# Attention sums kept by feature: denominators by DMA, the scaling on GpSimd, maxima turned by DVE

## Chip, cores and metric

The kernel runs on one core of a Trainium2 chip. The metric is the device time of one execution in microseconds.

## What is computed

A layer of attention and a recurrence, each followed by a residual sum and a layer norm, on x of shape (16, 512, 256):

```python
q = heads(x @ Wq); k_s, v_s = heads(x @ Wkv_short); k_l, v_l = heads(x @ Wkv_long)   # 16 heads of 16
decay_bias = -abs(pos[None, :] - pos[:, None]) * (1.0 - decay_factor)
out_short = attention(q, k_s, v_s, decay_bias)      # softmax(q k^T / 4 + bias) v
out_long = attention(q, k_l, v_l, None)
alpha = sigmoid(mix_weight)
x = layernorm(x + (alpha * out_short + (1 - alpha) * out_long) @ Wo)
# then, over the first axis t as time:
f = sigmoid(x_t @ wf.T + c @ uf.T + bf); i = sigmoid(x_t @ wi.T + c @ ui.T + bi); g = tanh(x_t @ wc.T + c @ uc.T + bc)
c = f * c + i * g
h = tanh(x @ wo.T + c_final @ uo.T + bo); x = layernorm(x + h)
```

## The kernel before

Attention comes first, for 16 batches b, then the recurrence. All five engines run orders written out by hand; they meet at semaphores. SP issues DMAs, GpSimd (POOL) has few instructions.

A batch is 8 units of 4 heads: unit u is head group u // 2 and attention u % 2 (0 long, 1 short). Units with u odd have the decay bias, whose diagonal part are small bf16 matmuls (L634). A unit is four slots of 128 keys, so a batch has 32 slots. In slot s PE computes the transposed scores for the exp ("b" fills, L658, in two pairs of heads), the scores of two units later, only for their row maxima ("a" fills, L684), weighs the values of the slot before with the exps (weigh, L722, sums and denominators in pv_ps, 17 rows per head: 16 features and the sum of exps), and may do a work task. ACT reads each "b" fill (exp, L391), DVE each "a" fill (maximum, L581). The fills of a unit go round three pairs of PSUM banks in the order FILLS (L107); before a fill PE waits until the fill three places back has been read (banks_free, L637). In the text b(2,0) is the "b" fill of the unit's third slot, first pair, and exp(2,0) the exp of it.

Work tasks (TASKS, L54) use the one bank `work`: "v" projects values, "kq" keys and queries (two halves; for the next batch), "wo" projects the attention output and DVE adds it to x_res (add_rows, L555), "ot" turns o_sum (L775), "turn" at slots 4m + 1. The turn of unit u - 1 transposes pv_sb, which ACT has copied from pv_ps (keep_sums, L424, after exp(0,1) of a unit), so that tokens lie on partitions; DVE takes the reciprocal of the denominators (L547) and multiplies (L551) into o_att. The same task turns the maxima of the next unit (L792); DVE negates them (L541) and SP writes them as an extra row of q_op (L304). GpSimd adds the two attentions' halves (o_sum, L332), twice per batch. "ot" makes the high part ot_h (ACT, L402) and the low part ot_l (DVE, L532), from which "wo" is made with three matmuls per product.

SP's order per batch: at slots 4m six DMAs with keys (load_k), at slots 8n + 2 six with queries (load_q), at slots 4m + 1 the maxima. GpSimd also makes xt_l, the low part of the next x (L339), which the kq tasks from slot 10 on and the x load on ACT at slot 10 (L434) wait for, and the factors of the layer norm (L345 to L350). After the last batch (L845 to L857) the first products of the recurrence are placed among the last steps of attention.

## Time and profile before

| | us |
|---|---|
| median of 3 runs | 2189.14 (2188.74 to 2189.32) |
| the profiled execution | 2190.01 |
| its span in the profile | 2188.2 |
| PE busy | 2107.5 (96%) |
| DVE busy | 1633.3 (75%) |
| ACT busy | 1470.2 (67%) |
| POOL busy | 134.4 (6%) |

The profile is of one execution. Busy time is the union of an engine's instructions; matmuls overlap, so the distance from one start to the next says what one costs. PEld are PE's weight loads. The idle time in front of an instruction stands in brackets with what released it. "SPq" and "ACTq" rows are DMA issues.

### The profile page before, as it was taken

How to read it: one execution, taken by the hardware profiler on the slowest of the kernel's cores; microseconds unless marked ns; L12 is line 12 of the kernel's file. 1: busy time of each engine (PE TensorE's matmuls, PEld its weight loads, DVE VectorE, ACT ScalarE, POOL GpSimd, SP SyncE). 2: the span in 40 equal slices, each digit the busy share in tenths (PEclk: the TensorE clock that was granted, in tenths of full speed). 3: DMA queues.
4: the chain of work that ended last, by engine and by line, in shares of the span. 5: the costliest groups of instructions: out<-in, count | busy, mean ns of one | idle time of the engine just before them, and what ended most of it. 6: DMA issues, size and time to landing. Idle time of an engine off the chain costs nothing.

```text
span 2188.2 us, 41691 instructions
## 1 busy us (share of the span) xinstructions
PE 2107.5 (96%) x16608; PEld 1139.3 (52%) x16608; DVE 1633.3 (75%) x2099; ACT 1470.2 (67%) x1766; POOL 134.4 (6%) x186
## 2 busy tenths in 40 slices
PE   6999999999999999999999999999999879999995
PEld 3444444444444444444444444444444348888873
DVE  6788888888888888888888888888888833333347
ACT  2777777777777777777777777787777653333338
POOL 0000000000000000000000000000000000000005
PEclk8999999999999999999999999999999989999998
DMA  4222222222222222222222222222222302000007
GB/s 109 55 57 55 67 55 66 55 64 55 65 56 66 56 65 56 64 56 64 56 63 64 55 64 55 64 55 64 55 55 54 91 28 69 29 20 28 29 10 259
DMA packets 91252, 134.14 MB, mean 61 GB/s; under 512 B 21301, under 2 KB 43573, under 8 KB 91077
## 3 DMA queue, kind: packets, MB, share of 16 engines
q1 hardware_dynamic: 66948, 97.91, 17.6%
q10 hardware_dynamic: 24128, 33.79, 4.8%
q8 instruction: 122, 2.00, 0.4%
q14 instruction: 54, 0.43, 0.1%
HBM read 37.77 MB, written 16.78 MB: 25 GB/s over the span
## 4 chain that ended last, share of the span: by engine, by line
PE 89%; ACT 4%; DVE 3%; issue 2%; DMA 1%; SPq 1%; ACTq 0%; POOL 0%; DVEq 0%; POOLq 0%
PE pv_ps L722 21%; PE pair_ps L658 17%; PE work L626 15%; PE banks L1176 12%; PE pair_ps L684 12%; PE work L788 3%; PE pair_ps L634 3%; ACT probs L391 2%; PE banks L1199 2%; DVE maxes L581 1%; PE banks L1233 1%; PE banks L1169 1%; PE work L792 1%; DVE res L563 1%; ACT summed L1044 1%
## 5 line engine op out<-in xcount | busy, mean ns | idle before, releaser
L581 DVE TENSOR_REDUCE maxes<-pair_ps 128x2 f32<-128x1024 f32 x1024 | 1228.0, 1221 | 240.5 <-PE pair_ps L634 153.9
L391 ACT ACTIVATE probs<-pair_ps,small 128x1024 f32<-128x1024 f32 x512 | 563.1, 1113 | 227.1 <-PE pair_ps L634 225.6
L391 ACT ACTIVATE probs<-pair_ps 128x1024 f32<-128x1024 f32 x512 | 516.8, 1024 | 160.0 <-PE pair_ps L658 154.8
L722 PE MATMUL pv_ps<-probs,vals 128*32 128x512 f32 x4096 | 547.3, 606 | 0.6 <-ACT probs L391 0.6
L658 PE MATMUL pair_ps<-q_op,k_op 56*128 56x512 f32 (+1 forms) x2048 | 479.6, 477 | 15.4 <-ACT probs L391 11.5
L684 PE MATMUL pair_ps<-k_op,q_op 55*128 55x512 f32 x2048 | 434.1, 432 | 6.7 <-ACT probs L391 4.5
L658 PEld LDWEIGHTS pair_ps<-q_op,k_op 56*128 56x128 f32 (+1 forms) x2048 | 191.7, 184 | 446.9 <-DVE maxes L581 204.7
L684 PEld LDWEIGHTS pair_ps<-k_op,q_op 55*128 55x128 f32 x2048 | 196.0, 186 | 151.4 <-issue 107.3
L634 PE MATMUL pair_ps<-eye_b,tri_b 64*128 64x64 bf16 x4096 | 163.0, 194 | 0.0
L634 PEld LDWEIGHTS pair_ps<-eye_b,tri_b 64*128 64x128 bf16 x4096 | 93.8, 96 | 114.6 <-issue 93.3
L722 PEld LDWEIGHTS pv_ps<-probs,vals 128*32 128x32 f32 x4096 | 80.7, 108 | 98.3 <-issue 87.3
L332 POOL TENSOR_TENSOR o_sum<-o_att 128x512 f32<-128x512 f32 x32 | 41.2, 1287 | 1287.9 <-DVE o_att L551 1287.9
L993 ACT ACTIVATE act_out<-banks,bias 128x512 f32<-128x512 f32 x96 | 65.9, 687 | 76.7 <-PE banks L1176 75.9
L1084 DVE TENSOR_TENSOR xs_l<-banks,xs_h 128x512 fp32r<-128x512 f32 x32 | 20.6, 685 | 104.8 <-ACT xs_h L982 104.8
L788 PE MATMUL work<-ident_sb,pv_sb 128*128 128x128 f32 x512 | 84.3, 288 | 14.3 <-ACT pv_sb L427 10.1
L626 PE MATMUL work<-xt_h,w_hi 128*128 128x512 f32 x184 | 92.6, 503 | 0.0
L427 ACT ACTIVATE pv_sb<-pv_ps 128x512 f32<-128x512 f32 x128 | 76.6, 598 | 22.3 <-PE pv_ps L722 15.3
L626 PE MATMUL work<-wv_hi,xt_h 128*128 128x256 f32 x256 | 84.7, 331 | 4.7 <-DVE w_lo L513 3.3
L982 ACT ACTIVATE xs_h<-banks 128x512 fp32r<-128x512 f32 x32 | 17.4, 595 | 105.2 <-PE banks L1169 105.2
L532 DVE SCALAR_TENSOR_TENSOR kq_l<-work,kq_h 128x512 fp32r<-128x512 f32 x92 | 63.6, 691 | 29.4 <-ACT kq_h L406 29.4
L1176 PE MATMUL banks<-xs_h,wx_h 128*128 128x512 f32 x192 | 76.1, 396 | 2.1 <-DVE xs_l L1084 2.1
L1176 PE MATMUL banks<-s_h,uc_h 128*128 128x512 f32 x192 | 77.4, 403 | 0.0
(161 smaller groups left out, 2450.5 us busy)
## 6 DMA issues: line engine op xcount, KB each, us to landing
k_op<-kq_h SPq DMA_DIRECT2D x508, 64.0 KB, 2.2
q_op<-kq_h SPq DMA_DIRECT2D x256, 64.0 KB, 2.2
k_op<-kq_l SPq DMA_DIRECT2D x254, 64.0 KB, 2.2
x_step<-in_xT ACTq DMA_DIRECT2D x16, 512.0 KB, 3.9
q_op<-kq_l SPq DMA_DIRECT2D x128, 64.0 KB, 2.2
x_res<-in_x ACTq DMA_DIRECT2D x16, 512.0 KB, 4.0
x_dram<-res ACTq DMA_DIRECT2D x16, 512.0 KB, 2.9
x_back<-x_dram SPq DMA_DIRECT2D x16, 512.0 KB, 5.4
```

The source lines that it names most:

```text
L391: act.activation(probs[:, s % 2, 2 * hp:2 * hp + 2, :], pairs_ps[pair_of(b, s, "b", hp)][:, :, :], ACT.Exp, scale=LAM if s // 4 % 2 else 1 ...
L427: act.activation(pv_sb[:, u % 2, :], pv_ps[:, :], ACT.Copy).then_inc(pv_copied, 1)
L532: dve.scalar_tensor_tensor(dst, work[:, :], scale, hi.bitcast(F32), ALU.mult, ALU.subtract).then_inc(done[kind], 1)
L581: dve.reduce_max(maxes[:, u % 2, :, hp, s % 4], pairs_ps[pair_of(b, s, "a", hp)][:, :, :], mybir.AxisListType.X).then_inc(a_reduced, 1)
L626: last = pe.matmul(out, lhs(a, k), rhs(c, k), start=(k == 0 and a + c == 0), stop=(k == KC - 1 and c == 1))
L634: yield pe.matmul(bank[:, P * chunk + HALF * half:P * chunk + HALF * half + HALF], tri_b[at:at + HALF, which, half, :], eye_b[at:at + HALF ...
L658: last = pe.matmul(banks[:, j, :], k[HALF * j:HALF * j + rows, hp, P * c:P * c + P], q[HALF * j:HALF * j + rows, hp, :], start=True, stop= ...
L684: last = pe.matmul(banks[:, j, :], q[at:at + MAX_ROW, hp, P * c:P * c + P], k[at:at + MAX_ROW, hp, :], start=True, stop=u % 2 == 0)
L722: last = pe.matmul(pv_ps[32 * h:32 * h + 32, :], vals[:, c, g // 2, att, at:at + 32], probs[:, s % 2, h, :], start=(c == 0), stop=(c == TC ...
L788: last = pe.transpose(work[:, P * t:P * t + P], pv_sb[:, sums[1] % 2, P * t:P * t + P], id_sb[:, :])
L993: act.activation(act_out[:, k, g, :], gate_ps[n], ACT.Tanh, bias=bias[:, g, k:k + 1], scale=0.5 if g < 2 else 1.0).then_inc(gate_done, 1)
L1176: last = pe.matmul(gate_ps[n], lhs[a][:, g, k, P * mc:P * mc + P], rhs[d][:, k, :], start=start and m == 0, stop=stop and m == len(parts) - 1)
```

## The change

Sums and denominators stay with features on partitions. pv_sb is copied from pv_ps as before; SP then moves its rows: the four denominators of a unit to `dens` (spread over 128 partitions, 16 each), the rows of each head to `o_att`, which is now laid out by feature: five DMAs per unit. Once per half batch (k = 0 or 1) DVE takes the reciprocal of dens (slots 3 and 19), SP stores it to DRAM (slots 4 and 20) and loads it back, each head's row repeated on 16 partitions, as `inverses` (two DMAs, slots 6 and 22). GpSimd multiplies o_att by it for both attentions and adds them to o_sum; ACT copies o_sum to ot_h (slots 9 and 25), GpSimd subtracts for ot_l. The task "ot" and the transposes of pv_sb are gone. The maxima of a unit are turned by DVE (32x32 blocks), in slot 4m, and moved by four DMAs instead of one; their sign is in the constants. PE's task "turn" is gone. "wo" stands at slots 12, 16, 20, "v" at 24, 28, 0, 2, 3, 4, 6. GpSimd's order per batch: multiply and add for k = 1 of the batch before, xt_l, ot_l for k = 1, layer norm factors, multiply and add and ot_l for k = 0. The memset of vals moves to GpSimd, the constants tri and eye are loaded into x_res.

```diff
-TASKS = {0: ("ot", 0, -1), 2: ("v", (4,), 0), 3: ("v", (5,), 0), 4: ("v", (6,), 0), 6: ("ot", 1, -1), 7: ("v", (7,), 0),
-         8: ("wo", (0,), -1), 12: ("wo", (1,), -1), 16: ("wo", (2, 3), -1), 20: ("v", (0, 1), 1), 24: ("v", (2,), 1), 28: ("v", (3,), 1)}
+TASKS = {0: ("v", (3,), 0), 2: ("v", (4,), 0), 3: ("v", (5,), 0), 4: ("v", (6,), 0), 6: ("v", (7,), 0),
+         12: ("wo", (0,), -1), 16: ("wo", (1,), -1), 20: ("wo", (2, 3), -1), 24: ("v", (0, 1), 1), 28: ("v", (2,), 1)}
 TASKS |= {10 + 4 * i + half: ("kq", (n, half), 1) for i, n in enumerate(KQ_ORDER) for half in range(2)}
 
-TASKS |= {4 * m + 1: ("turn", m, 0) for m in range(UNITS)}
+
+INVERT, STORE_INVERSES, LOAD_INVERSES, HIGH_PART = ({at: (1, -1), at + 16: (0, 0)} for at in (3, 4, 6, 9))
...
-        rden = sb("rden", [P, 2, TC, GH])
-        o_att = [sb(f"o_att{a}", [P, TC, NH, HD]) for a in range(2)]
-        o_sum = sb("o_sum", [P, TC, H])
+
+        o_att, inverses = sb("o_att", [P, 2, KC, L]), sb("inverses", [P, 2, L])
+        o_sum = sb("o_sum", [P, KC, L])
+
+        dens = sb("dens", [P, KC, 2, 2, HD])
+        inv_dram = nc.dram_tensor("inv_dram", [KC, 2, 2, GH * L], F32, kind="Internal").ap()
...
-        maxes = sb("maxes", [P, 2, 2, GH // 2, TC])
-        shift_rows = sb("shift_rows", [GH * TC, 2, P], F32R)
-
-        tri_sb, tri_b = sb("tri_sb", [P, 2, 2, P]), sb("tri_b", [P, 2, 2, P], BF16)
-        eye_sb, eye_b = sb("eye_sb", [P, HALF]), sb("eye_b", [P, HALF], BF16)
+        maxes = sb("maxes", [P, 2, 2 * GH * TC], F32R)
+        maxima = [maxes[:, a, 0:GH * TC].rearrange("p (h m c) -> p h m c", h=2, m=GH // 2) for a in range(2)]
+
+        shift_rows = sb("shift_rows", [P, 2, 2 * GH * TC], F32R)
+
+        tri_b, eye_b = sb("tri_b", [P, 2, 2, P], BF16), sb("eye_b", [P, HALF], BF16)
+        x_res_flat = x_res[:, :, :].rearrange("p t n -> p (t n)")
+        tri_sb = x_res_flat[:, 0:4 * P].rearrange("p (a f n) -> p a f n", a=2, f=2)
+        eye_sb = x_res_flat[:, 4 * P:4 * P + HALF]
...
+            def move_maxima(b, u):
+                if exists(b):
+                    wait(sp, done["shift"], b, UNITS, u + 1)
+                    row = MAX_ROW + u % 2
+                    to = q_op[u // 2][row:row + HALF + 1:HALF, :, :].rearrange("r h (t n) -> r (h t) n", n=P)
+                    for at in range(0, P, 32):
+                        copy_words(to[:, :, at:at + 32], shift_rows[at:at + GH * TC, u % 2, :]).then_inc(shift_loaded[u % 2], 16)
+
+            def move_sums(b, u):
+
+                if exists(b):
+                    g, att = u // 2, u % 2
+                    wait(sp, pv_copied, b, UNITS, u + 1)
+                    wait(sp, inv_stored, b, 16 * 2, 16 * (u // 4 - 1))
+                    sp.dma_start(dens[:, g // 2, att, g % 2, :], pv_sb[HD:P:32, att, :]).then_inc(sums_moved[att], 16)
+                    wait(sp, osum_done, b, 2, u // 4 - 1)
+                    for h in range(GH):
+                        to = HALF * (g % 2) + HD * h
+                        sp.dma_start(o_att[to:to + HD, att, g // 2, :], pv_sb[32 * h:32 * h + HD, att, :]).then_inc(sums_moved[att], 16)
+
+            def store_inverses(b, k):
+                if exists(b):
+                    wait(sp, inverted, b, 2, k + 1)
+                    for a in range(2):
+                        wait(sp, inv_loaded[a], b, 16 * 2, 16 * (k - 1))
+                    sp.dma_start(inv_dram[k].rearrange("a g (p e) -> p (a g) e", p=P), dens[:, k, :, :, :].rearrange("p a g e -> p (a g) e")).then_inc(inv_stored, 16)
+
+            def load_inverses(b, k):
+                if exists(b):
+                    wait(sp, inv_stored, b, 16 * 2, 16 * (k + 1))
+                    for a in range(2):
+                        wait(sp, scaled, b, 4, 2 * k)
+                        rows = inv_dram[k, a].rearrange("g (h n) -> (g h) n", n=L)
+                        sp.dma_start(inverses[:, a, :], rows.unsqueeze(1).to_broadcast([2 * GH, HD, L])).then_inc(inv_loaded[a], 16)
...
-                    if s in TASKS and TASKS[s][0] == "turn":
-                        _, maxima = turned(b, TASKS[s][1])
-                        if maxima:
-                            bb, u = maxima
-                            wait(sp, done["shift"], bb, UNITS, u + 1)
-                            row = MAX_ROW + u % 2
-                            copy_words(q_op[u // 2][row:row + HALF + 1:HALF, :, :].rearrange("r h (t n) -> r (h t) n", n=P),
-                                       shift_rows[:, u % 2, :]).then_inc(shift_loaded[u % 2], 16)
+                    if s % 4 == 1:
+                        move_maxima(*unit_of(b, s // 4 + 1))
+                        move_sums(*sums_before(b, s // 4))
+                    for slots, move in ((STORE_INVERSES, store_inverses), (LOAD_INVERSES, load_inverses)):
+                        if s in slots:
+                            k, off = slots[s]
+                            move(b + off, k)
...
+            move_sums(B - 1, UNITS - 1)
+            store_inverses(B - 1, 1)
+            load_inverses(B - 1, 1)
...
+            pool.memset(vals[:, :, :, :, :], 1.0).then_inc(ones_set, 1)
+            pool.memset(maxes[:, :, :].bitcast(F32), 0.0).then_inc(ones_set, 1)
...
-                def add_attentions(bb, n):
-
-                    wait(pool, done["pvt"], bb, UNITS, UNITS // 2 * (n + 1))
-                    o = [a[:, :, NH // 2 * n:NH // 2 * (n + 1), :].rearrange("p t h d -> p t (h d)") for a in o_att]
-                    pool.tensor_tensor(o_sum[:, :, P * n:P * n + P], o[0], o[1], ALU.add).then_inc(osum_done, 1)
+                def add_attentions(bb, k):
+
+                    for a in range(2):
+                        wait(pool, inv_loaded[a], bb, 16 * 2, 16 * (k + 1))
+                        pool.tensor_tensor(o_att[:, a, k, :], o_att[:, a, k, :], inverses[:, a, :], ALU.mult).then_inc(scaled, 1)
+                    wait(pool, scaled, bb, 4, 2 * k + 2)
+                    wait(pool, done["ot"], bb, 2, k - 1)
+                    pool.tensor_tensor(o_sum[:, k, :], o_att[:, 0, k, :], o_att[:, 1, k, :], ALU.add).then_inc(osum_done, 1)
+
+                def low_part(bb, k):
+                    wait(pool, ot_hi, bb, 2, k + 1)
+                    wait(pool, full["wo"], bb, 4, 0)
+                    pool.tensor_tensor(ot_l[:, k, :], o_sum[:, k, :], ot_h[:, k, :].bitcast(F32), ALU.subtract).then_inc(done["ot"], 1)
...
                                        ALU.subtract).then_inc(xt_lo, 1)
-                if exists(b):
-                    add_attentions(b, 0)
+                if exists(bb):
+                    low_part(bb, 1)
...
                 wait(act, pv_full, b, SLOTS, 4 * u + 4)
+                wait(act, sums_moved[u % 2], b, 80 * UNITS // 2, 80 * (u // 2))
                 act.activation(pv_sb[:, u % 2, :], pv_ps[:, :], ACT.Copy).then_inc(pv_copied, 1)
+
+            def high_part(b, k):
+
+                if exists(b):
+                    wait(act, osum_done, b, 2, k + 1)
+                    wait(act, full["wo"], b, 4, 0)
+                    act.activation(ot_h[:, k, :], o_sum[:, k, :], ACT.Copy).then_inc(ot_hi, 1)
...
+                    if s in HIGH_PART:
+                        k, off = HIGH_PART[s]
+                        high_part(b + off, k)
...
-            def turn(b, m):
-
-                sums, maxima = turned(b, m)
-                wait(dve, full["turn"], b, UNITS, m + 2)
-                if maxima:
-                    bb, u = maxima
-                    wait(dve, shift_loaded[u % 2], bb, 16 * UNITS // 2, 16 * (u // 2))
-                    dve.tensor_scalar(shift_rows[:, u % 2, :].rearrange("p (g e) -> p g e", e=GAP), turned_maxima, -1.0, None,
-                                      ALU.mult).then_inc(done["shift"], 1)
-                if sums:
-                    bb, u = sums
-                    g, att = u // 2, u % 2
-                    o = work[:, :].rearrange("p (t h e) -> p t h e", t=TC, h=GH)
-                    dve.reciprocal(rden[:, att, :, :], o[:, :, :, HD]).then_inc(rden_done, 1)
-                    wait(dve, rden_done, bb, UNITS, u + 1)
-                    if u < 2:
-                        wait(dve, osum_done, bb, 2, 0)
-                    dve.tensor_tensor(o_att[att][:, :, GH * g:GH * g + GH, :], o[:, :, :, 0:HD],
-                                      rden[:, att, :, :].unsqueeze(3).to_broadcast([P, TC, GH, HD]),
-                                      ALU.mult).then_inc(done["pvt"], 1)
+            def turn(b, u):
+
+
+                if exists(b):
+                    wait(dve, a_reduced, b, 8 * UNITS, 8 * u + 8)
+                    wait(dve, shift_loaded[u % 2], b, 64 * UNITS // 2, 64 * (u // 2))
+                    dve.transpose(shift_rows[:, u % 2, :].bitcast(F32), maxes[:, u % 2, :].bitcast(F32)).then_inc(done["shift"], 1)
+
+            def invert(b, k):
+
+                if exists(b):
+                    for a in range(2):
+                        wait(dve, sums_moved[a], b, 80 * UNITS // 2, 80 * (2 * k + 2))
+                    dve.reciprocal(dens[:, k, :, :, :], dens[:, k, :, :, :]).then_inc(inverted, 1)
...
+                        turn(*unit_of(b, s // 4 + 1))
                         reduce(1)
...
+                    if s in INVERT:
+                        k, off = INVERT[s]
+                        invert(b + off, k)
...
-            after.prepare(dve)
-            rest(ot_l[:, 0, :], ot_h[:, 0, :], ot_hi, "ot", B - 1, 0, 1.0)
-            turn(B, 0)
             after.step_lo(dve, 0, 0)
             after.step_lo(dve, 0, 1)
-            rest(ot_l[:, 1, :], ot_h[:, 1, :], ot_hi, "ot", B - 1, 1, 1.0)
+            invert(B - 1, 1)
+            after.prepare(dve)
...
-                    wait(pe, osum_done, bb, 2, n + 1)
-                    for t in range(TC):
-                        last = pe.transpose(work[:, P * t:P * t + P], o_sum[:, t, P * n:P * n + P], id_sb[:, :])
-                    last.then_inc(full["ot"], 1)
                 if kind == "wo":
                     wait(pe, done["ot"], bb, 2, 2)
                     for t in n:
                         at = H * (t % 2)
                         three(work[:, at:at + H], lambda a, k: (ot_h, ot_l)[a][:, k, P * t:P * t + P],
                               lambda a, k: (w_hi, w_lo)[a][:, 3, k, :]).then_inc(full["wo"], 1)
...
-                if kind == "turn":
-                    sums, maxima = turned(b, n)
-                    if sums:
-                        wait(pe, pv_copied, sums[0], UNITS, sums[1] + 1)
-                        for t in range(TC):
-                            last = pe.transpose(work[:, P * t:P * t + P], pv_sb[:, sums[1] % 2, P * t:P * t + P], id_sb[:, :])
-                    if maxima:
-
-                        wait(pe, a_reduced, maxima[0], 8 * UNITS, 8 * maxima[1] + 8)
-                        last = pe.transpose(turned_maxima, maxes[:, maxima[1] % 2, :, :, :].rearrange("p a h t -> p (a h t)"), id_sb[:, :])
-                    last.then_inc(full["turn"], 1)
 
...
-            work_task(B, 0)
             weigh_before(B, 0)
             after.turn_step(pe, 0, True)
-            work_task(B, 1)
-            after.gates_from_x(pe, 0, (0, 1), True)
-            work_task(B, 6)
-            after.gates_from_x(pe, 0, (2, 3), True)
+            after.gates_from_x(pe, 0, (0, 1, 2, 3), True)
             pe.wait_ge(done["ot"], 2 * B)
             for t in range(TC):
```

## Rows read from the trace of the kernel before

**Rows 1.** The page's fourth part: the chain that ended last, its shares by engine.
```profile
PE 89%; ACT 4%; DVE 3%; issue 2%; DMA 1%; SPq 1%; ACTq 0%; POOL 0%; DVEq 0%; POOLq 0%
```

**Rows 2.** Busy time by stretches (one batch; before the recurrence): columns in its header.
```profile
core 0: us, PE busy (x) PEld busy (x) DVE busy (x) ACT busy (x) POOL busy (x), PEclk, DMA share, GB/s
697.25:805.40 108.15, 107.17 (x928) 51.65 (x926) 90.68 (x108) 81.41 (x93) 6.54 (x7) 1.00 0.24 60
1770.00:1800.00 30.00, 22.20 (x134) 15.34 (x131) 12.34 (x31) 8.05 (x12) 2.05 (x3) 0.81 0.06 18
```

**Rows 3.** Timeline, slot 5: start us, length us, engine, line, operation, tiles, count.
```profile
930.07 2.12 ACT L391 ACTIVATE probs<-pair_ps,small 128x1024 f32<-128x1024 f32 x2 [0.17 <-PE pair_ps L634]
930.34 0.66 PE L788 MATMUL work<-ident_sb,pv_sb 128*128 128x128 f32 x4
...
931.03 1.06 PE L722 MATMUL pv_ps<-probs,vals 128*32 128x512 f32 x8
...
932.73 0.47 PE L684 MATMUL pair_ps<-k_op,q_op 55*128 55x512 f32 x2
```

**Rows 4.** Timeline, slot 9, a unit without bias.
```profile
943.77 1.21 DVE L581 TENSOR_REDUCE maxes<-pair_ps 128x2 f32<-128x1024 f32 x1
...
944.42 1.02 ACT L391 ACTIVATE probs<-pair_ps 128x1024 f32<-128x1024 f32 x1
...
945.31 0.50 PE L658 MATMUL pair_ps<-q_op,k_op 56*128 56x512 f32 x2
...
945.65 0.63 PE L684 MATMUL pair_ps<-k_op,q_op 55*128 55x512 f32 x4
```

**Rows 5.** Timeline, slot 17, behind the double wo task; in brackets idle time and releaser.
```profile
972.85 0.50 PE L658 MATMUL pair_ps<-q_op,k_op 56*128 56x512 f32 x2 [0.15 <-DVE maxes L581]
```

**Rows 6.** The chain in order of time (two pieces), then timeline rows of fills that wait.
```profile
913.93 0.59 PE work L775 x4
...
926.46 0.90 PE work L626 x6
...
934.04 0.50 PE L658 MATMUL pair_ps<-q_op,k_op 57*128 57x512 f32 x2 [0.18 <-ACT probs L391]
...
1749.19 0.50 PE L684 MATMUL pair_ps<-k_op,q_op 55*128 55x512 f32 x2 [0.83 <-ACT probs L391]
```

**Rows 7.** Groups of instructions by line: the shift_rows step.
```profile
L541 DVE TENSOR_SCALAR shift_rows<-work 16x128 fp32r<-16x128 f32 x128 | 35.0, 273 | 8.7 <-PE work L792 8.6
```

**Rows 8.** SP: timeline; issues of q_op (ns min/median/max); page part 6 (us to landing).
```profile
912.22 2.47 SPq L238 DMA_DIRECT2D k_op<-kq_h  x4
...
L238 SPq DMA_DIRECT2D q_op<-kq_h x256: 564/592/1917, 17.0 to 1704.8; - x128
...
L243 SPq DMA_DIRECT2D q_op<-shift_rows x128: 495/539/584, 41.5 to 1755.5; - x128
...
k_op<-kq_h SPq DMA_DIRECT2D x508, 64.0 KB, 2.2
...
x_res<-in_x ACTq DMA_DIRECT2D x16, 512.0 KB, 4.0
x_dram<-res ACTq DMA_DIRECT2D x16, 512.0 KB, 2.9
...
weights_as_they_are<-in_uo SPq DMA_DIRECT2D x1, 256.0 KB, 5.8
```

**Rows 9.** Groups of instructions by line: GpSimd's two large operations.
```profile
L332 POOL TENSOR_TENSOR o_sum<-o_att 128x512 f32<-128x512 f32 x32 | 41.2, 1287 | 1287.9 <-DVE o_att L551 1287.9
...
L339 POOL TENSOR_TENSOR xt_l<-x_step,xt_h 128x1024 fp32r<-128x1024 f32 x15 | 35.7, 2378 | 147.6 <-ACT xt_h L433 147.6
```

**Rows 10.** Timeline of the end of attention.
```profile
1778.02 0.60 ACT L427 ACTIVATE pv_sb<-pv_ps 128x512 f32<-128x512 f32 x1 [0.18 <-PE pv_ps L722]
...
1794.50 0.28 PE L626 MATMUL work<-w_hi,ot_h 128*128 128x256 f32 x1
...
1798.24 0.39 PE L1199 MATMUL banks<-wo_h,xs_h 128*128 128x256 f32 x1 [0.74 <-DVE res L563]
```

63 lines of the change are left out of this document (23 added, 40 removed).

## Prediction

> **What bounds the kernel now.** I read the chain that ended last first: TensorE (PE) holds 89% of it [rows 1]. Then the table by stretches, for exactly one batch in the steady state: 108.15 us, of which PE is busy 107.17, DVE 90.68, ACT 81.41, GpSimd (POOL) 6.54, at a full clock [rows 2]. Sixteen such batches make up attention, up to about 1778 us; the recurrence behind it is not touched. So PE time taken out of a batch shows in the span, but only as far as ACT and DVE, at 75% and 84%, can deliver at the new pace. The three PSUM pairs couple them: each fill by PE must wait until ACT (exp) or DVE (max) has read the fill three places back in FILLS. So I read the timeline around every step that goes, and asked how much slack the next fills had.
>
> **What goes from PE.** Eight blocks per batch at slots 4m+1 (four transposes of pv_sb, one of maxes): from the start of the L788 group to the start of the next weigh block is 931.03 - 930.34 = 0.69 us [rows 3]; 8 x 0.69 = 5.5 us. Two blocks of four o_sum transposes, 0.59 us each in the chain, and one of them is followed by a wait of 0.18 us on an exp [rows 6]: together 1.4 us. Were that all, a batch would fall by 6.9 us to 101.3.
>
> **What the bank ring takes back.** After the block come weigh and the fills b(2,0), a(1,1), a(2,0). a(2,0) needs the bank that exp(1,1) reads, and this exp follows the copy of pv_ps on ACT, which the change leaves where it is.
> Units with bias: that exp ends at 930.07 + 2.12 = 932.19, a(2,0) starts at 932.73 [rows 3]. Slack 0.54; PE would come 0.69 earlier, so 0.15 and some 0.05 of start-up come back: 0.2.
> Units without: the exp ends at 944.42 + 1.02 = 945.44; the row at 945.65 holds two pairs, of which a(2,0) is the second, 0.23 later [rows 4]. Slack 0.44: 0.3 comes back. Over eight units that is 2.0 us.
> Where DVE adds residual rows (wo tasks, now slots 12, 16, 20), b(2,0) is late instead. The max ends at 943.77 + 1.21 = 944.98 and b(2,0) starts 945.31, a slack of 0.33 [rows 4]: 0.1 more than counted at slot 16. With the double task PE waits for DVE already [rows 5], so at slot 20 all of the 0.69 comes back: 0.5 more. Ring: 2.6 us per batch.
>
> **What moving the tasks does.** wo moves from 8, 12, 16 to 12, 16, 20, v from 7 to 6, so slots 7 and 8 have no task. A v or kq task is 0.90 us of PE [rows 6]. In the last batch, which has slots without tasks, PE stands idle 0.83 us for ACT there [rows 6]: two fills without a task between them (the row at 1749.19) come faster than the exp of the first. So slot 7 gives back 0.83, slot 8 (no bias, shorter exps) about 0.6: 1.4 us, as much as the o_sum transposes gave.
>
> **ACT.** The copies to ot_h come from SBUF, behind exp(1,1) at slots 9 and 25. I price one at 0.60 us, like the 128x512 copy at 1778.02 [rows 10]. exp(2,0) would then end at 945.44 + 0.60 + 1.02 = 947.06, while PE wants b(2,1) at 945.65 + 0.56 + 0.90 - 0.69 + 0.3 = 946.7 [rows 4, 6]: 0.35 lost. At slot 25 a normalise of the same size stands ahead of it: 0.95. Together 1.3 us. The x_res load of slot 21 now waits for the rows that slot 20 adds, with exp(21,0) queued behind it; some 0.2 us, hidden by the 0.7 that b(2,0) waits there anyway. The memset that moves to GpSimd and the constants that move into x_res lie in the first 27 us, beside weight loads, and cost nothing; a slow memset there would delay the first maxima once.
>
> **DVE.** The reciprocal on 128x16, the multiply and the shift_rows step go, 8 times each, and ot_l twice; a 128x32 transpose comes 8 times and a 128x64 reciprocal twice. The shift_rows step is 273 ns [rows 7]; the transpose reads and writes SBUF with fewer elements, so between 0.1 and 0.3, and it stands where DVE waits for PE between two maxima. I take nothing for it. The reciprocal follows the last maximum of slots 3 and 19; between 0.2 and 0.7 us, the next maximum has room for some 0.4 of idle time: 0 to 0.3 per case, I take 0. The reciprocal of slot 3 also waits for the sums, with the maxima of slot 4 queued behind it; they are issued by 921.3 (see SP) and 2.2 us later landed, at 923.5, while slot 3's last maximum ends after 924: covered. If SP were 2 us later, DVE and with it PE would stand. DVE as a whole is relieved by about 5 us per batch and still binds nothing.
>
> **SP and the new chain.** SP issues 80 DMAs per batch now (48 for keys, 24 for queries, 8 for maxima); the change makes it 150: 24 more for maxima, 40 for sums, 6 for the inverses. One issue is 0.54 to 0.59 us [rows 8], 0.6 with its gap: 90 us of 107. SP keeps up, but late. Followed through from slot 0, where it starts on the keys at 912.2 [rows 8]: 6 keys, 4 maxima, 5 sums, 6 queries, 6 keys, 1 store, 4 maxima, 5 sums are 37 issues, 22.5 us. Its waits ahead of these are over by then: the last unit's pv_sb is copied 4 us after slot 0, the store's reciprocal is done in slot 3. The loads of inverses go out at 934.7 and 935.3. They are 256 KB each; I take 4.0 us to landing from x_res (512 KB from DRAM) and 1.6 more for the second: 938.7 and 940.3. The lower bound is 2.2 (64 KB, SBUF to SBUF), the upper 5.8 (256 KB of weights from DRAM) [rows 8]. The store (2.9 us like x_dram [rows 8]) lands long before.
> Then GpSimd: three operations of 1287 ns, and only behind them xt_l with 2378 ns, which in GpSimd's order stands behind them [rows 9]. xt_l is done at 940.3 + 1.3 + 1.3 + 2.4 = 945.3. It used to be done by slot 5; its readers are the kq task of slot 10 and, on ACT, the x load ahead of exp(10,0). By the sums above that task comes at 945.0. It waits 0.3, ACT's exp too: 0.6 in all. With the landing at its bounds it is 0 and about 2.5 us per batch. The queued work behind ACT's wait is every exp of slot 10, and PE waits for these.
>
> The Trainium skill, page "DMA: Bandwidth & Descriptors", section "Anatomy of one DMA", fits a DMA at about 2.0 us plus bytes over 436 GB/s, which for 256 KB makes an estimated 2.6 us. By that the inverses land 1.4 us earlier, xt_l has no reader waiting, and the total would be about 9 us lower. The row for x_res, 4.0 us [rows 8], is nearer in kind and I go by it.
>
> **The end.** The last unit's sums have nothing to hide behind. From the end of the pv_ps copy (1778.62) to the first recurrence block after the residual (1798.24) it is 19.6 us now, of which wo and rows are 1798.24 - 1794.50 = 3.7 [rows 10]. After: five issues 2.6, landing 2.2, reciprocal 0.4, store 0.6 + 2.9, two loads 0.6 + 4.0 and some for the second, three on GpSimd 3.9, ot_h 0.7, ot_l on GpSimd 1.3, wo and rows 3.7: about 23.5. PE meanwhile can do the first gates and then idles some 8 us; this stretch shows a granted clock of 0.81 already [rows 2], and a slower start of the recurrence may add 2. So +6, between +2 and +10.
>
> **The sum.** Per batch -5.5 - 1.4 + 2.6 + 1.4 + 1.3 + 0.6 = -1.0 us. Fifteen batches: -15 or, with the small DVE terms I left at zero (0 to 0.6 per batch, say 0.15), -13. The last batch, whose last units wait for ACT anyway, -1. End +6. Total -8 on a span of 2188.2 us; the execution with that profile took 2190.0, the median of the runs is 2189.1. Forecast: 2181 us.
>
> **Rivals.**
> Full relief: the ring waits don't come, because exps and maxima start earlier too. PE then keeps its 6.9 us: 15.5 x 6.9 = 107, with the end 2189 - 107 + 6 = 2088. For it: the busy shares of ACT and DVE. Against: the exps behind the pv_ps copy run back to back [rows 3, 4], and the slots without tasks show the wait [rows 6]. Half of it would be about 2135.
> A new wait: xt_l reaches its readers late. Place: GpSimd's order behind the inverses' round trip through DRAM. It decides once the loads land more than about 1 us later than I take; each us more costs 15. At 5.8 us landing, or issues of 0.75 us, it is 2.5 to 4 us per batch: 2181 + 15 x 3 = 2226, slower. For it: an issue can take 1917 ns [rows 8].
> No relief: ring waits 0.1 larger than taken in each unit and the end at +10, both within what my reading of starts and ends can tell: 2181 + 15 x 8 x 0.1 + 4 = 2197.
>
> **How the numbers follow.** A measurement of this kernel tells a change from none at about 0.2%, or 4.4 us: 2184.8 to 2193.5 is "same". The forecast's own case, 2165 to 2193, has 0.45, a fifth of it in "same"; full or half relief 0.17; late xt_l 0.25; no relief 0.13, partly in "same". Faster 0.50, same 0.19, slower 0.31. The range leaves out the far half of the relief and the tail of the late wait: 2145 to 2230.
>
> **What would show it.** PE's L788, L792, L775 gone and the batch period from 108.15 to about 107; waits at L658 and L684 on ACT L391 grown to about 6 us per batch; idle time at the fill behind slots 7 and 8; the reader of xt_l waiting under 0.5 us; SP issuing some 90 us per batch; some 23 us between the last copy and the recurrence. Wrong if a batch comes below 104 (no ring waits) or above 109 (late xt_l, or SP behind).

## The result and the profile after

The change makes the kernel slower: 2262.15 us median (2259.60 to 2263.61), against 2188.94 for the kernel before. The ratio is 1.0335, with a 95% interval from 1.0317 to 1.0353. The forecast was 2181 us, with a range up to 2230: wrong in sign and outside the range.

The profiled execution of the changed kernel has a span of 2261.8 us, 73.6 more than before. The head of its page, busy time and share:

```profile
span 2261.8 us, 41351 instructions
PE 2067.0 (91%) x15840; PEld 1078.9 (48%) x15840; DVE 1546.3 (68%) x1842; ACT 1470.2 (65%) x1766; POOL 257.1 (11%) x284
PE 54%; SPq 16%; issue 7%; ACT 7%; DVE 5%; POOL 5%; DMA 5%; ACTq 1%; DVEq 0%; POOLq 0%
```

The third line is the chain of waits. It was 89% PE [rows 1]; now SP's queue, GpSimd and the DMAs hold 26% of it. The table by stretches for one batch, to be set beside [rows 2] (columns as there: length, busy time of PE, PEld, DVE, ACT and POOL, then the granted clock as a share of 2.4 GHz, DMA share, GB/s):

```profile
912.80:1025.60 112.80, 104.99 (x881) 47.80 (x880) 86.00 (x92) 82.04 (x94) 14.62 (x14) 0.97 0.32 78
```

PE does its work in 105.0 us instead of 107.2, as meant, although some of it runs at a lower clock; it idles 7.8 us where it idled 1. The clock is 0.97 where it was 1.00. ACT's copy to xt_h happens once per batch, so its first and last start give the mean batch. First the kernel before, then after:

```profile
L433 ACT ACTIVATE xt_h<-x_step x15: 1049/1049/1051, 62.4 to 1574.3; 128x1024 fp32r<-128x1024 f32 x15
```

```profile
L491 ACT ACTIVATE xt_h<-x_step x15: 1049/1049/1049, 61.9 to 1630.8; 128x1024 fp32r<-128x1024 f32 x15
```

Divided by 14 that is 107.99 and 112.06 us: +4.07 per batch, where I had -1.0. "Mean batch" below always means this. The first of the 14 intervals is unlike the rest: at slot 10 of batch 0 there are no sums of an earlier batch that could be late. It ends with the second copy, before and after:

```profile
168.27 1.05 ACT L433 ACTIVATE xt_h<-x_step 128x1024 fp32r<-128x1024 f32 x1
```

```profile
165.63 1.05 ACT L491 ACTIVATE xt_h<-x_step 128x1024 fp32r<-128x1024 f32 x1
```

So the first interval fell from 105.9 to 103.8 us, and the other thirteen ("later batches" below) rose from 108.16 to 112.71 on the mean, +4.55. The +4.07 accounts for 57 of the 73.6 us; from that copy to the last copy of pv_ps it is another 11.2 (the last such batch and the batch behind it), and from there to the end 5.9.

Where in the batch? PE, ACT and GpSimd around slot 10, from the timeline (start, duration, engine, line, tiles, then in brackets the idle time before it and what ended it). PE:

```profile
978.84 0.77 PE L677 MATMUL work<-xt_h,w_hi 128*128 128x512 f32 x1 [3.62 <-POOL xt_l L389]
981.54 1.93 PE L773 MATMUL pv_ps<-probs,vals 128*32 128x512 f32 x8
```

ACT, which waits twice, for o_sum at slot 9 and for xt_l at slot 10:

```profile
976.43 0.63 ACT L485 ACTIVATE ot_h<-o_sum 128x512 fp32r<-128x512 f32 x1 [1.76 <-POOL o_sum L377]
979.25 1.02 ACT L444 ACTIVATE probs<-pair_ps 128x1024 f32<-128x1024 f32 x1 [2.20 <-POOL xt_l L389]
```

GpSimd, in its own order:

```profile
971.49 1.27 POOL L374 TENSOR_TENSOR o_att<-o_att,inverses 128x512 f32<-128x512 f32 x1 [47.07 <-DMA inverses<-inv_dram]
973.77 1.28 POOL L374 TENSOR_TENSOR o_att<-o_att,inverses 128x512 f32<-128x512 f32 x1 [1.01 <-DMA inverses<-inv_dram]
975.13 1.26 POOL L377 TENSOR_TENSOR o_sum<-o_att 128x512 f32<-128x512 f32 x1
976.35 2.34 POOL L389 TENSOR_TENSOR xt_l<-x_step,xt_h 128x1024 fp32r<-128x1024 f32 x1
```

And the table by stretches over the same time:

```profile
974.00:976.00 2.00, 1.07 (x6) 0.33 (x6) 1.39 (x2) 0.67 (x1) 1.92 (x2) 1.00 0.07 11
976.00:978.00 2.00, 0.00 (x0) 0.00 (x0) 0.97 (x1) 0.63 (x1) 2.00 (x2) 0.91 0.22 49
978.00:980.00 2.00, 1.16 (x3) 0.83 (x3) 0.00 (x0) 0.75 (x1) 1.93 (x2) 0.50 0.61 108
982.00:984.00 2.00, 2.00 (x12) 0.50 (x4) 0.88 (x1) 0.25 (x1) 0.00 (x0) 0.50 0.65 169
986.00:988.00 2.00, 2.00 (x23) 0.75 (x22) 1.83 (x3) 1.11 (x3) 0.00 (x0) 1.00 0.14 37
```

PE stands still for 3.6 us, and then the granted clock is 0.50, the 1.2 GHz level, until 984 to 986: a weigh block of eight matmuls takes 1.93 us where it takes 1.06 at full clock. The list of waits puts the same in sums over the whole run (us in total, times, the longest):

```profile
PE work L677 <- POOL xt_l L389: 58.4, 14, 5.4
ACT probs L444 <- POOL xt_l L389: 28.7, 13, 2.2
ACT ot_h L485 <- POOL o_sum L377: 51.0, 18, 15.3
```

The first row is 4.2 us on the mean, so the 3.6 us of the batch shown is a short one; of the 51.0 us in the last row 15.3 are one wait at the end of attention. That is the rival "late xt_l". SP reaches the loads late:

```profile
942.20 2.49 SPq L241 DMA_DIRECT2D k_op<-kq_h  x4
958.46 2.01 SPq L241 DMA_DIRECT2D k_op<-kq_l  x2
966.68 1.35 SPq L318 DMA_DIRECT2D inverses<-inv_dram  x2
```

The keys of slot 0 start at 942.20 and the loads at 966.68, 24.5 us later.

### The profile page after: what moved, and what is told of

It reads as the page before. It is cut to its first block, busy times and chain, and to the rows that moved or that the text cites. A ratio compares the mean times of both kernels' runs of the same rounds, so it can differ in the third digit from the quotient of the medians.

```text
span 2261.8 us, 41351 instructions
## 1 busy us (share of the span) xinstructions
PE 2067.0 (91%) x15840; PEld 1078.9 (48%) x15840; DVE 1546.3 (68%) x1842; ACT 1470.2 (65%) x1766; POOL 257.1 (11%) x284
## 3 DMA queue, kind: packets, MB, share of 16 engines
q1 hardware_dynamic: 132740, 133.61, 24.3%
## 4 chain that ended last, share of the span: by engine, by line
PE 54%; SPq 16%; issue 7%; ACT 7%; DVE 5%; POOL 5%; DMA 5%; ACTq 1%; DVEq 0%; POOLq 0%
PE banks L1200 12%; PE work L677 11%; PE pair_ps L709 10%; PE pv_ps L773 10%; SPq L241 8%; PE pair_ps L735 7%; ACT probs L444 5%; DMA inverses<-inv_dram 4%; SPq L303 3%; SPq L246 3%; DVE maxes L634 2%; PE banks L1223 2%; POOL o_att L374 2%; PE pair_ps L685 2%; POOL xt_l L389 1%
## 5 line engine op out<-in xcount | busy, mean ns | idle before, releaser
L634 DVE TENSOR_REDUCE maxes<-pair_ps 128x2 fp32r<-128x1024 f32 x1024 | 1232.8, 1222 | 399.1 <-PE pair_ps L735 226.1
L773 PE MATMUL pv_ps<-probs,vals 128*32 128x512 f32 x4096 | 563.1, 623 | 10.9 <-ACT pv_sb L478 10.9
L709 PE MATMUL pair_ps<-q_op,k_op 56*128 56x512 f32 (+1 forms) x2048 | 488.3, 485 | 36.7 <-ACT probs L444 20.2
L735 PE MATMUL pair_ps<-k_op,q_op 55*128 55x512 f32 x2048 | 457.6, 446 | 39.3 <-ACT probs L444 25.9
L735 PEld LDWEIGHTS pair_ps<-k_op,q_op 55*128 55x128 f32 x2048 | 200.6, 191 | 213.4 <-issue 105.9
L374 POOL TENSOR_TENSOR o_att<-o_att,inverses 128x512 f32<-128x512 f32 x64 | 81.8, 1279 | 866.1 <-DMA inverses<-inv_dram 866.1
L677 PE MATMUL work<-xt_h,w_hi 128*128 128x512 f32 x184 | 97.9, 532 | 58.4 <-POOL xt_l L389 58.4
L677 PEld LDWEIGHTS work<-xt_h,w_hi 128*128 128x128 f32 x184 | 36.5, 198 | 95.0 <-issue 90.3
```

The lines of the kernel that those rows point to most:

```text
L374: pool.tensor_tensor(o_att[:, a, k, :], o_att[:, a, k, :], inverses[:, a, :], ALU.mult).then_inc(scaled, 1)
L634: dve.reduce_max(maxima[u % 2][:, :, hp, s % 4], pairs_ps[pair_of(b, s, "a", hp)][:, :, :], mybir.AxisListType.X).then_inc(a_reduced, 1)
L677: last = pe.matmul(out, lhs(a, k), rhs(c, k), start=(k == 0 and a + c == 0), stop=(k == KC - 1 and c == 1))
L709: last = pe.matmul(banks[:, j, :], k[HALF * j:HALF * j + rows, hp, P * c:P * c + P], q[HALF * j:HALF * j + rows, hp, :], start=True, stop= ...
L735: last = pe.matmul(banks[:, j, :], q[at:at + MAX_ROW, hp, P * c:P * c + P], k[at:at + MAX_ROW, hp, :], start=True, stop=u % 2 == 0)
L773: last = pe.matmul(pv_ps[32 * h:32 * h + 32, :], vals[:, c, g // 2, att, at:at + 32], probs[:, s % 2, h, :], start=(c == 0), stop=(c == TC ...
```

## Experiments

All times are medians, each with its ratio to the kernel before, measured beside it.

**e1: xt_l out of the queue behind the inverses.**

```diff
 # gpsimd, body
+                <the subtraction that makes xt_l of batch b + 1>
                 if exists(bb):
                     add_attentions(bb, 1)
-                <the subtraction that makes xt_l of batch b + 1>
```

> The changed kernel with one thing moved: on GpSimd xt_l now stands ahead of the scaling of the batch before, not behind it. Theory (late xt_l, then a cold clock): TensorE waits 3.6 us for xt_l at slot 10 of each of 15 batches and then runs some 6 us at a granted clock of 0.5, which costs about 3.3 us more. Both go. But ACT still waits for o_sum at slot 9 (1.8 us in the trace), so exp(10,0) is about 2 us late and PE waits that long for its bank, at a full clock: 112.8 - 3.6 - 3.3 + 2.0 = 107.9 us per batch, about 2190 us in all. Rival (the bank ring and SP, not xt_l, make the kernel slow): the wait moves to the next fill and the total stays above 2240.

Measured: 2247.09 us, ratio 1.0268 [1.0239, 1.0297]. Neither 2190 nor unchanged: 15 us. In its trace xt_l is done at 952.8, and nobody waits for it any more. ACT waits instead, one slot earlier:

```profile
969.81 1.27 POOL L377 TENSOR_TENSOR o_sum<-o_att 128x512 f32<-128x512 f32 x1
```

```profile
971.11 0.63 ACT L485 ACTIVATE ot_h<-o_sum 128x512 fp32r<-128x512 f32 x1 [2.42 <-POOL o_sum L377]
976.41 1.03 ACT L444 ACTIVATE probs<-pair_ps 128x1024 f32<-128x1024 f32 x1 [2.00 <-PE pair_ps L709]
```

The exps of slots 9 and 10 are queued behind that copy and PE waits for them, long enough for the clock to fall again (PE busy time is the first number behind the length):

```profile
970.00:972.00 2.00, 0.14 (x1) 0.00 (x0) 1.01 (x1) 0.89 (x2) 1.26 (x2) 1.00 0.24 47
974.00:976.00 2.00, 2.00 (x10) 0.43 (x4) 1.05 (x1) 0.42 (x1) 0.00 (x0) 0.50 0.96 255
```

The lists of waits have it for the whole run, the kernel after first, then e1 (PE's 58.4 us for xt_l are gone in e1):

```profile
PE pair_ps L709 <- ACT probs L444: 20.2, 24, 3.5
```

```profile
PE pair_ps L709 <- ACT probs L444: 60.4, 37, 3.6
```

So the same lateness reached PE by two ways, xt_l and o_sum, and to take one away frees only the difference between them. What is late is the inverses.

**e2: PE kept busy while it waits.**

```diff
 # tensor, work_task
                 work_free(b, s)
+                if s == 10 and b >= 0 and exists(bb):
+                    for _ in range(16):
+                        pe.matmul(work[:, :], w_hi[:, 0, 0, 0:P], xt_h[b % 2][:, 0, :], start=True, stop=True)
                 if kind in ("kq", "v"):
                     wait(pe, xt_lo, bb, 1, 1)
```

> The changed kernel, with 16 matmuls of 512 columns that compute nothing needed, put in front of the wait for xt_l at slot 10, in PE's free bank. They take about 3.7 us, as long as the wait. Theory (the idle wait lets the clock fall, and that is half of the loss): the wait stays as long, but the granted clock stays at 1.0 behind it, and a batch falls from 112.8 to about 109.5, the total to about 2212 us. Rival (the clock falls for another reason, or a cold clock costs nothing there because ACT and DVE set the pace): total within 5 us of 2262.

Measured: 2246.47 us, ratio 1.0262 [1.0241, 1.0283]. The wait is as long as before, but the clock stays at 1.00 all through it, and the mean batch is 111.03 us: 1.03 less. That figure is too low for the clock, because the 16 matmuls also stand in batch 0, which has no wait for them to fill:

```profile
86.34 4.01 PE L804 MATMUL work<-xt_h,w_hi 128*128 128x512 f32 x16
```

The first interval is 110.2 us there instead of 103.8. The later batches are 111.09 instead of 112.71, so 1.6 less. The expectation of 3.3 took the stretched durations for lost time. In this trace the first fill after slot 10 does not start when PE is ready but waits for an exp that itself came late:

```profile
979.66 0.50 PE L709 MATMUL pair_ps<-q_op,k_op 56*128 56x512 f32 x2 [0.62 <-ACT probs L444]
```

Half of the price of the low clock is real. Of the other half this row shows 0.6 us as hidden behind ACT; for the rest that is argued. Against e8 below, in which nothing is late (106.12 us), a later batch of the kernel after costs 6.6 us more: the idling some 5, and the clock 1.6.

**e3: the turns alone, out of the kernel before.** This kernel leaves out the transposes of the sums and of the maxima and shifts the exps by a constant, so it does not compute the layer; it only measures time.

```diff
 # tensor: the "turn" task
-                    <4 transposes of pv_sb and one of maxes into work>
-                    last.then_inc(full["turn"], 1)
+                    pass
 # vector: the step that waits for full["turn"] waits for pv_copied and a_reduced instead
```

> The kernel before, without the turn block on PE: no transposes of pv_sb and of the maxima (DVE's steps stay and read what the bank holds; the shift of the exps is a constant -30; the attention sums are not the reference's). Measures alone what PE gets back for 8 x 0.69 us per batch. Theory (the bank ring takes 40% back, by the slack at each unit): 3.0 us per batch, total about 2189 - 49 = 2140 us, with new waits at L658 and L684 for ACT L391 in the slot behind each turn. Rival (full relief): 5.5 us per batch, total about 2101 us.

Measured: 2141.70 us, ratio 0.9786 [0.9768, 0.9803]; the theory's 2140. The mean batch is 105.01, so 2.98 less for 5.5 us of PE work taken out: the bank ring takes 2.5 back, where the sum had 2.6. The waits at the two fills say where. First the kernel before (PEld is PE's weight load, which waits on behalf of the matmul), then this one:

```profile
PEld pair_ps L658 <- DVE maxes L581: 204.7, 243, 1.4
PEld pair_ps L684 <- ACT probs L391: 7.1, 8, 1.1
```

```profile
PEld pair_ps L663 <- DVE maxes L586: 237.9, 258, 1.8
PEld pair_ps L689 <- ACT probs L391: 32.5, 101, 1.2
```

The waits for the maxima grew by 33 us and those for the exps at L689 by 25, where the sum had 2.0 of its 2.6 us on the exps: the size came out right, the place only in part.

**e4: only the loads of the inverses, earlier in SP's order.**

```diff
 # sync, body
                     if s % 4 == 1:
+                        if s in (5, 21):
+                            load_inverses(b - (s == 5), int(s == 5))
                         move_maxima(*unit_of(b, s // 4 + 1))
                         move_sums(*sums_before(b, s // 4))
-                    <load_inverses at slots 6 and 22>
```

> The changed kernel, with the two loads of inverses issued at slots 5 and 21 ahead of that slot's nine DMAs, not at 6 and 22 behind them. SP then waits about 2 us for the store to land, but the loads go out some 3.5 us earlier. Theory (late xt_l, then a cold clock): the inverses land 3.5 us earlier, xt_l is done about when PE asks for it, a batch falls to about 106 us, the total to about 2163 us. Rival (GpSimd itself or the DMA rings, not SP's order, make the inverses late): under 1 us per batch, total above 2245.

Measured: 2178.19 us, ratio 0.9947 [0.9930, 0.9965]. To move two DMAs ahead of nine others is worth 84 us; lateness is the cause, and the kernel is now faster than before. It is 15 us short of the 2163 expected, though the later batches, at 106.44 us, are near the 106 expected: the expected 99 us are 15 times what one batch of 112.8 us loses on the way to 106.2, while PE has the wait in 14 batches and the later ones fell by 6.3 on the mean. There is also a new wait. SP waits at the load for the store to land, and the maxima queued behind the load come late for PE, 9 times and 9.4 us in all:

```profile
979.46 0.50 PE L711 MATMUL pair_ps<-q_op,k_op 56*128 56x512 f32 x2 [1.38 <-DMA q_op<-shift_rows]
```

**e5: GpSimd issues the store and the loads itself.**

```diff
-            def store_inverses(b, k): ...   # on SP, called at slots 4 and 20
-            def load_inverses(b, k): ...    # on SP, called at slots 6 and 22
+            <the same two functions, with pool in place of sp>
                 def add_attentions(bb, k):
+                    store_inverses(bb, k)
+                    load_inverses(bb, k)
```

> The changed kernel, but the store and the two loads of the inverses are issued by GpSimd, which idles for some 90 us of each batch, instead of by SP. They then go out as soon as the reciprocal is done (slots 3 and 19) and no longer stand in SP's order with the keys and maxima. In the run with the loads earlier in SP's order (108.4 us per batch) PE still waits 1.4 us for the q_op rows of the maxima that stand behind the loads, and there are other such bits. Theory (the lateness of the inverses is the loss, and SP's order is why they are late): no wait for xt_l or o_sum, no wait for q_op, a batch of about 107: 2155 us (2140 to 2170). Rival (what is left in the run with early loads is the bank ring and the empty slots, not SP): 2178, as that run. Second rival (DMAs issued by GpSimd land much later): above 2200.

Measured: 2260.57 us, ratio 1.0325 [1.0308, 1.0343]. A miss of 105 us, and no rival's mechanism either. At slot 10 all is well: the multiplies begin 24.3 us after SP's keys of slot 0 (23.9 in e4, 29.3 in the kernel after). But GpSimd's order is one queue too. The store and loads for the first half of the heads, whose reciprocal is done at 1010.5, stood behind the layer-norm steps:

```profile
1021.03 0.20 POOL L390 TENSOR_TENSOR veps<-mv,consts 128x4 f32<-128x4 f32 x1 [42.13 <-DVE mv L619]
1023.12 0.86 POOL L353 DMA_DIRECT2D inv_dram<-dens  x1 [0.31 <-issue]
1026.30 1.21 POOL L361 DMA_DIRECT2D inverses<-inv_dram  x2 [2.32 <-DMA inv_dram<-dens]
1033.11 1.26 POOL L372 TENSOR_TENSOR o_sum<-o_att 128x512 f32<-128x512 f32 x1
```

and the loss of slot 10 came back whole at slot 25, again by way of ACT's copy:

```profile
1034.40 0.63 ACT L480 ACTIVATE ot_h<-o_sum 128x512 fp32r<-128x512 f32 x1 [3.44 <-POOL o_sum L372]
```

```profile
1036.00 0.79 PE L704 MATMUL pair_ps<-q_op,k_op 56*128 56x512 f32 x2 [4.08 <-ACT probs L439]
```

**e6: the same with one task moved.** The v task of slot 6 goes back to slot 7.

```diff
-TASKS = {..., 6: ("v", (7,), 0),
+TASKS = {..., 7: ("v", (7,), 0),
```

> As the run in which GpSimd issues the store and the loads of the inverses, but the v task of slot 6 goes back to slot 7, so that slots 6 and 8 stand empty instead of 7 and 8, with a task between them. By the prediction's term for empty slots (PE gives back 0.8 and 0.6 us where fills follow each other without a task between them) an empty slot costs the same wherever it stands: within 3 us of the other run. Rival (two empty slots in a row cost more than two apart, as ACT's backlog adds up over them): 8 to 12 us faster.

Measured: 2260.23 us, ratio 1.0328 [1.0311, 1.0345], against 2260.57. An empty slot costs the same beside another empty one as apart from it, in a kernel that has e5's wait at slot 25 in either case.

**e7: xt_l later still.**

```diff
 # gpsimd: the subtraction that makes xt_l
-                                       ALU.subtract).then_inc(xt_lo, 1)
+                                       ALU.subtract).then_inc(xt_twice, 1)
+                    wait(pool, xt_twice, b + 1, 1, 0)
+                    <the same subtraction once more>.then_inc(xt_lo, 1)
```

> The changed kernel with the GpSimd subtraction that makes xt_l done twice, one after the other, so that xt_l is done 2.4 us later in each of 15 batches; the same numbers are written. Theory (PE at slot 10 waits for xt_l, each us of its lateness is a us per batch): 2262 + 15 x 2.4 = 2298, and 10 us more if the clock stays low for longer. Rival (by slot 10 PE has lost what it loses to the o_sum wait of ACT at slot 9, and xt_l is only the name in the record): under 2275.

Measured: 2298.93 us, ratio 1.0509 [1.0491, 1.0526]. The theory's 2298; the mean batch is 114.57, 2.51 more for 2.4 us of lateness. The later batches grow by 2.7 us and PE's wait by 2.8 (from 4.2 to 7.0 on the mean):

```profile
PE work L680 <- POOL xt_l L392: 97.4, 14, 7.7
```

In the range in which it is late, xt_l costs a microsecond per microsecond, and the longer idling costs no more clock.

**e8: e5 with the right order.**

```diff
 # gpsimd, body: the calls leave add_attentions; those for (bb, 1) stand first in the order
+                store_inverses(b, 0)
+                load_inverses(b, 0)
                 if exists(bb):
                     wait(pool, mv_done, bb, TC, TC)
```

> As the run in which GpSimd issues the store and the loads of the inverses, but in GpSimd's order those of the slots 19 (first half of the heads) now stand ahead of the layer-norm steps, which wait for the last residual rows of slot 20. In the run before, slot 10 no longer waited for xt_l (the multiplies began 24.5 us after kq_l of slot 0, as in the run with the loads earlier), but the batch lost the same again at slot 25, where ACT's copy to ot_h waited for an o_sum that stood behind the layer-norm steps; PE idled 4 us there and its granted clock fell. Theory: with both halves on time a batch is 106.5 to 107.5, 2150 to 2165 us. Rival (the run with early loads already has all there is): 2178. Rival (GpSimd's DMAs or its busy spans harm something else): above 2200.

Measured: 2168.06 us, ratio 0.9903 [0.9886, 0.9919], 3 us above the range of the theory. The mean batch is 105.91:

```profile
L488 ACT ACTIVATE xt_h<-x_step x15: 1049/1049/1050, 62.5 to 1545.3; 128x1024 fp32r<-128x1024 f32 x15
```

**e9: GpSimd also makes ot_h.**

```diff
 # gpsimd, add_attentions
+                    wait(pool, full["wo"], bb, 4, 0)
+                    pool.tensor_tensor(ot_h[:, k, :], o_att[:, 0, k, :], o_att[:, 1, k, :], ALU.add).then_inc(ot_hi, 1)
                     <o_sum as before>
 # scalar, body
-                    if s in HIGH_PART: <high_part>
 # gpsimd, body: xt_l between store_inverses(bb, 1) and load_inverses(bb, 1)
```

> As e8, and the two copies to ot_h per batch leave ACT: GpSimd adds the two attentions twice, once into ot_h (rounded to the narrow type) and once into o_sum, then subtracts; xt_l comes between the store and the loads. By the prediction's ACT term (1.3 us per batch for the two copies, 0.35 and 0.95) this is worth 15 x 1.3 = 20 us over e8; one more GpSimd addition of 1.3 us lies where GpSimd idles. Rival (ACT has room there, since the fills behind it wait for DVE or PE): within 4 us of e8. The end grows by about 0.6 us in either case.

Measured: 2159.53 us, ratio 0.9865 [0.9848, 0.9881]: 8.5 us less than e8, between the 20 of the theory and the 4 of the rival. The mean batch falls by 0.58, where the ACT term had 1.3.

**e10: the recurrence's weights leave SP.** In e9 a wait showed in the last batch that neither kernel had. SP issues 12 DMAs for the recurrence (three of them in the first row, the last at 1677.47) and then the maxima of the next unit:

```profile
1670.93 1.58 SPq L329 DMA_DIRECT2D weights_as_they_are<-in_wx  x3
1677.97 2.23 SPq L246 DMA_DIRECT2D q_op<-shift_rows  x4
```

```profile
1682.87 0.50 PE L705 MATMUL pair_ps<-q_op,k_op 56*128 56x512 f32 x2 [3.23 <-DMA q_op<-shift_rows]
```

```diff
 # sync, at slot 12 of the last batch
-                        for at, w in zip(self.stages, (wx[0], wx[1], wx[2], wo, uc[0], uc[1], uc[2], uo)):
-                            sp.dma_start(at, by_rows(w)).then_inc(shared.weights_in, 16)
 # gpsimd, body(B - 1), behind low_part(bb, 1): the same loop with pool
```

> As e9, and the eight weight loads for the recurrence, which SP issues at slot 12 of the last batch, are issued by GpSimd instead. In e9's trace SP issues 13 such DMAs from 1671.5 to 1677.9 us and only then the q_op rows of the maxima for the next unit; PE waits 3.23 us for them at 1682.87 and runs at a granted clock of 0.50 from 1684 on. In the kernel before, maxima were turned on TensorE and moved by 2 DMAs after the same loads, and PE did not wait there. Theory: the last batch gets the wait and the slow clock back, 4 to 6 us: 2154. Rival (GpSimd's issues take longer and the weights land in the way of the maxima all the same): within 1.5 us of e9, 2160.

Measured: 2154.92 us, ratio 0.9844 [0.9830, 0.9857], 4.6 less than e9. The intervals of e9 and e10 overlap, so as a time this is not certain. In the traces PE has no wait for q_op there any more, and from the last copy to xt_h to the last copy of pv_ps it is 200.9 us instead of 206.8.

**e11: PE kept busy at the end.**

```diff
 # tensor, behind the last batch
+            pe.wait_ge(done["wo"], 4 * (B - 1))
+            for _ in range(48):
+                pe.matmul(work[:, :], w_hi[:, 0, 0, 0:P], w_hi[:, 0, :, :].rearrange("p k n -> p (k n)"), start=True, stop=True)
             pe.wait_ge(done["ot"], 2 * B)
```

> As e10, and PE does 48 more matmuls of 128x512 (results unused) while it waits, in e9 for 12.0 us, for the last ot_l. In e9 the granted clock is 0.50 in the last 4 us of that wait and through the 24 matmuls of the last output projection, which take 5.3 us. Theory (the clock falls because PE idles): the clock stays at 1.00, the projection takes 2.8 us and the whole is 2.5 to 3 us less than e10. Rival (the clock there is set by something else, or the added matmuls outlast the wait): the same as e10 or more.

Measured: 2151.94 us, ratio 0.9837 [0.9821, 0.9852]. The intervals of e10 and e11 overlap, so the 3.0 us between the medians are not certain as a time. The trace shows it at the spot. The stretch behind PE's wait for the last ot_l in e10, then in e11:

```profile
1760.00:1764.00 4.00, 4.00 (x21) 4.00 (x20) 2.54 (x6) 0.00 (x0) 0.00 (x0) 0.50 0.00 0
```

```profile
1760.00:1764.00 4.00, 3.28 (x27) 3.08 (x27) 3.34 (x12) 0.00 (x0) 0.00 (x0) 1.00 0.00 0
```

From the end of the last copy of pv_ps to the first recurrence block behind the residual it is 26.2 us in e10 (1738.62 to 1764.85) and 24.3 in e11 (1739.06 to 1763.33). e11 has the lowest median of the versions that compute the whole layer.

**e12: work put into the empty slots.**

```diff
 # tensor, work_task
                 if not has_task(b, s):
+                    if s in (7, 8) and 0 < b < B - 1:
+                        work_free(b, s)
+                        for _ in range(4):
+                            pe.matmul(work[:, :], w_hi[:, 0, 0, 0:P], xt_h[b % 2][:, 0, :], start=True, stop=True)
                     return
```

> As e10, with four matmuls of 128x512 (results unused, 0.92 us of PE) in each of the empty slots 7 and 8 of batches 1 to 14. The prediction's term: without a task there PE idles for the exp 0.83 and 0.6 us, so the added work costs nothing up to that: 28 x (0.92 - 0.7) = 6 us more than e10, at most 8. Rival (an empty slot gives nothing back, PE's time there is PE's time): 28 x 0.92 = 26 us more.

Measured: 2166.01 us, ratio 0.9896 [0.9881, 0.9911]: 11.1 us more than e10 for 28 fills, or 0.40 each of 0.92 us of work. By that an empty slot gives back 0.52 on the mean. By the later batches, 106.11 us against 105.46 in e10, two fills cost 0.65 us and a slot gives back 0.59. The prediction had 0.83 and 0.6; the expectation of at most 8 is missed by 3.

## Why the prediction was wrong

**The step that failed** is the last one of the part on SP and the new chain: at slot 10 PE and ACT wait 0.3 us each for xt_l, "0.6 in all". PE's wait was 4.2 us on the mean. It had three faults.

First, a margin made of two large sums. The reader's side was right: PE arrives at slot 10 33.0 us after SP's keys of slot 0 (978.84 - 3.62 - 942.20), forecast 32.8. The supplier's side came out at 36.5 (978.69 - 942.20) and not 33.1. SP's 37 issues took 24.5 us instead of 22.5: two pairs of k_op loads took 1.8 and 2.0 us instead of 1.23, the rest is the gaps between groups. The landings took 4.8 us for the first load and 7.1 for the second, counted from the first issue to GpSimd's multiplies, instead of 4.0 and 5.6. The sum of 2.0 and 1.5 is all but the 3.6 us of the wait shown. The rival named its threshold rightly, 1 us beyond what I took for the loads. But two terms of one chain made 3.5 together, although neither was as bad as the rival's bounds (5.8 us landing, 0.75 us for an issue, against 4.8 and 0.66). A chance of 0.25 was too low for a margin of -0.3 us at the end of a chain of 33.

Second, the price. "Each us more costs 15" is right for one more microsecond while it is late (e7: 2.7 in a batch for 2.4, in 14 batches), but it is not the whole. From the kernel after to e8, in which nothing is late, it is 112.71 - 106.12 = 6.6 us in each of the later batches, of which PE's wait is 4.2 on the mean. The low clock behind it is 1.6 (e2). The remaining 0.8 or so I put down to ACT, which waited twice itself and comes out of the wait with its exps undone; e1 shows that its wait for o_sum is there by itself, but no run takes it away alone, so its share is argued. So the rival's 2226 should have been some 2260.

Third, one reader of two. The prediction followed xt_l to PE and ACT and priced ACT's copy to ot_h only by its own duration, not by when o_sum is there. o_sum stands 2.4 us ahead of xt_l in GpSimd's order, but its reader stands a slot earlier as well: ACT reached the copy 32.5 us after SP's keys (976.43 - 1.76 - 942.20), the forecast had o_sum at 30.7 by its own terms (940.3 + 2.6 - 912.2), and it came at 34.2. A slack of 1.8 us was thus gone before the lateness reached 3.5. e1 shows that this reader alone is enough for most of the loss, and e5 the same for its copy at slot 25; no run has xt_l as the only late one.

**What held.** The prediction's sign of being wrong, a batch above 109 us for a late xt_l, is what came. The rest of the sum can be read in e8: -2.1 us per batch (105.91 - 107.99), where the forecast without its lateness term had -1.6. The first interval of the kernel after, without a wait, shows the same -2.1. Point by point:
- Turns and ring: -5.5 + 2.6, measured -2.98 together (e3). "Full relief" is out.
- Empty slots: +1.4 forecast; 1.0 to 1.2 by e12 (2 x 0.52 or 2 x 0.59).
- ACT's copies: +1.3 forecast, 0.58 by e9, which also moved xt_l and added 1.3 us on GpSimd; so this is what the exchange brings, not a clean price.
- o_sum transposes: -1.4, not tested alone. The three terms above and this one sum to -2.98 - 1.4 + 1.0 + 0.6 = -2.8 (-2.6 with 1.2), against -2.1 measured: 0.5 to 0.7 per batch is unaccounted for. The small DVE steps that I had put at nothing (0.15 in the total) may be part of it; no run tests them.
- The end: +6 forecast, 5.9 measured. From the last copy's end to the recurrence it is 23.8 us in the kernel after (1846.35 to 1870.11), against 19.6 in [rows 10]; forecast 23.5.
- The last batch: -1 forecast. It has its own lateness in the kernel after (3.46 us of PE idle at 1766.77, 2.67 at 1824.26), and after that was cured in e8 and e9 the recurrence's weights on SP cost some 4.6 more (e10). I had not looked at that queue in the last batch, although the maxima now depend on SP four issues deep.
- DVE: the 128x64 reciprocal takes 541 ns, the 128x32 transpose 0.20 us; both within the bounds given.

The formula of the Trainium skill ("DMA: Bandwidth & Descriptors", section "Anatomy of one DMA"), by which 256 KB makes an estimated 2.6 us, is further off than my row: the loads took 4.8 us and more here. It would have led to a forecast still lower. That section gives it for DMAs that GpSimd issues, which the prediction passed over; but where GpSimd issues these loads (e8) they take 3.7 us at the least and 4.8 in the median.

The change does what it says: TensorE does less. It loses because what PE and DVE used to do in place became a round trip of SP's queue, a store, two loads and GpSimd. With the round trip issued by GpSimd in the right order, the same idea gives 0.9903 of the time before, and with what the traces showed next (e9 to e11) 0.9837.

## What to carry to other kernels

When work moves from the bound engine to a round trip, work out the slack of every reader of every result of the chain, not only the last one, and treat a margin of a few tenths at the end of a 30 us sum as a coin toss; then price the wrong side in full, with the clock and with the engines that were held up. A DMA that a later step waits for belongs ahead of the ones that nothing waits for yet, and an idle engine can issue it only if its own program order has no other wait in front. After each cure look for the next wait before forecasting the gain: e1, e4, e5 and e8 each gave less than was forecast for them. And look at the first batch by itself: an interval in which the wait cannot occur shows what the change is worth without it, and a mean over all batches hides it.
